# Taking the norms of q and k from squared slot-wise products, in an attention and expert kernel on one core

## The reference, cut to what matters

```python
def l2norm(t):
    n = jnp.linalg.norm(t, axis=-1, keepdims=True)
    return t / jnp.maximum(n, EPS)                       # EPS = 1e-12

q, k, v = (l2norm(q), l2norm(k), l2norm(v))              # 16 heads, DK = 16, DV = 64
attn = jnp.square(jax.nn.relu(jnp.einsum('bhid,bhjd->bhij', q, k)))
out = tanh_norm(jnp.einsum('bhij,bhjd->bhid', attn, v))  # tanh(n) * out / max(n, EPS)
return out.transpose(0, 2, 1, 3).reshape(b, n, h * d) @ Wout
```

## Time and profile before

| | |
|---|---|
| median of 3 runs | 552.65 us (552.19 to 552.93) |
| profiled execution, its own time | 551.87 us |
| its span in the trace | 549.8 us |
| busy: PE, DVE, ACT, POOL | 527.1, 425.2, 371.4, 331.3 us |
| attention | from 0 to about 219 us, then the experts |
| chain that ended last: PE, POOL, issue, DVE | 61%, 14%, 13%, 6% |

### The profile page before, as it was taken

One profiled execution on the slowest core, in us unless ns is written; L12 is line 12 of the kernel. 1 busy time (PEld: TensorE's weight loads), 2 busy tenths in 40 slices (PEclk: granted clock), 3 DMA queues, 4 the chain that ended last, 5 costly groups with the idle time before them and its releaser, 6 DMA issues.

```text
span 549.8 us, 10227 instructions
## 1 busy us (share of the span) xinstructions
PE 527.1 (96%) x3288; PEld 393.9 (72%) x3288; DVE 425.2 (77%) x1004; ACT 371.4 (68%) x682; POOL 331.3 (60%) x280
## 2 busy tenths in 40 slices
PE   8798899999999999898999999999999999999997
PEld 7565557676767666686878878878868878878884
DVE  5877868888978698669769778778769778777765
ACT  5697859687769786644565865865865865755654
POOL 6645919393947584395466655655655655665562
PEclk9899989999999999999999999999999999999999
DMA  7401010101010100660291760870760780771930
GB/s 218 131 2 30 1 30 1 32 1 30 2 31 1 30 2 9 171 148 2 77 209 30 184 153 4 176 156 11 184 151 4 182 175 5 170 159 35 214 83 20
DMA packets 37253, 44.75 MB, mean 81 GB/s; under 512 B 5840, under 2 KB 20304, under 8 KB 37200
## 3 DMA queue, kind: packets, MB, share of 16 engines
q1 hardware_dynamic: 32512, 42.40, 33.3%
q10 hardware_dynamic: 4688, 1.71, 1.3%
HBM read 40.94 MB, written 3.15 MB: 80 GB/s over the span
## 4 chain that ended last, share of the span: by engine, by line
PE 61%; POOL 14%; issue 13%; DVE 6%; ACT 4%; DMA 1%; SPq 0%; POOLq 0%; ACTq 0%; DVEq 0%
PE PS L1245 59%; POOL hl L517 11%; DVE aT L892 2%; ACT v L556 1%; POOL sr L446 1%; ACT rl L581 1%; DMA Osb<-wa_dram 1%; DVE n L871 1%; POOL mrstd L508 1%; POOL rstd L461 1%; DVE nmx L904 1%; ACT sqv L563 0%; POOL fxl L468 0%; DVE hb L1118 0%; PE PS L1338 0%
## 5 line engine op out<-in xcount | busy, mean ns | idle before, releaser
L517 POOL TENSOR_TENSOR hl<-hb,hh 128x512 fp32r<-128x512 f32 x127 | 164.3, 1295 | 129.2 <-ACT hh L735 124.9
L728 ACT ACTIVATE sil<-PS 128x512 f32<-128x512 f32 (+1 forms) x136 | 80.8, 595 | 79.0 <-PE PS L1245 72.4
L1113 DVE TENSOR_TENSOR PS<-sil,PS 128x512 f32<-128x512 f32 x128 | 88.3, 690 | 54.3 <-PE PS L1245 33.0
L1245 PE MATMUL PS<-fxh,wfh 128*128 128x512 f32 x264 | 104.9, 397 | 3.3 <-DVE hb L1118 2.9
L735 ACT ACTIVATE hh<-hb 128x512 fp32r<-128x512 f32 x128 | 80.3, 627 | 35.3 <-DVE hb L1118 33.4
L1245 PE MATMUL PS<-fxl,wfh 128*128 128x512 f32 x264 | 104.1, 394 | 0.0
L1245 PE MATMUL PS<-fxh,wfl 128*128 128x512 f32 x264 | 103.7, 393 | 0.0
L1118 DVE TENSOR_TENSOR hb<-PS,wbc 128x512 f32<-128x512 f32 x128 | 88.5, 691 | 12.9 <-issue 4.2
L892 DVE SCALAR_TENSOR_TENSOR aT<-PS,rl 128x1024 f32<-128x1024 f32 x64 | 75.2, 1216 | 14.7 <-ACT rl L581 14.6
L581 ACT ACTIVATE rl<-PS 128x1024 f32<-128x1024 f32 x64 | 62.8, 1050 | 21.7 <-PE PS L1245 21.7
L436 POOL TENSOR_TENSOR sr<-n2o,half 128x32 f32<-128x32 f32 x7 | 37.9, 5414 | 44.4 <-DVE n2o L899 44.4
(11 more groups left out here) (182 smaller groups left out, 900.1 us busy)
## 6 DMA issues: line engine op xcount, KB each, us to landing
wbc<-w_dram SPq DMA_DIRECT2D x48, 512.0 KB, 11.7
wbc<-w_dram SPq DMA_DIRECT2D x32, 128.0 KB, 3.0
wbc<-w_dram SPq DMA_DIRECT2D x16, 256.0 KB, 4.2
wfs<-wf_dram SPq DMA_DIRECT2D x32, 98.0 KB, 2.2
band_dram<-zero SPq DMA_DIRECT2D x16, 80.0 KB, 1.7
band<-band_dram ACTq DMA_DIRECT2D x4, 320.0 KB, 3.0
...
```

The lines of the kernel that those rows point to most:

```text
L517: g.tensor_tensor(hl[:, n % RING, :], hb[:, n % RING, :], hh[:, n % RING, :].bitcast(F32), ALU.subtract).then_inc(F("hl"), 1)
L728: s.activation(sil[0:rows, n % 2, :], PS[0:rows, G0 + n % 2, :], ACT.Silu).then_inc(F("silu"), 1)
L1113: v_.tensor_tensor(PS[:, bank, :], sil[:, n % 2, :], PS[:, bank, :], ALU.mult).then_inc(F("t"), 1)
L1245: return nc.tensor.matmul(o, w, m, start=start, stop=stop)
```

## The change

The token-wise second product of q and k is taken out, with its 512 columns of weights. The slot-wise products in `qk`, which are there anyway, are squared to a new buffer `sqg`: parts 0 and 1 by POOL (a multiplication of 128x512 each), part 2 by ACT. For the first batch DVE squares all three. PE's new `pair_sums(n)` adds them up over the rows of a head by eight matmuls with columns of ones (`indp`), into other columns of the same bank as the output's sums (`output_sums`, the former `norms`). One copy and one pair of transposes now carry the sums of q and k of batch n and of the outputs of batch n-2. `keep_norms` and `transpose_norms` therefore take the number n, and run once more at the start and once more at the end than before.

With that the order changes on every engine. PE's three `group` calls stand together after the first `score` of a pass; `values(n, 0, ...)` move one place later, `values(n, 1, ...)` to after the third `score`, `project(r, 0)` from before the third `score` to before the fourth. `qk` has two copies, so that a batch's parts may be written while the one before is in use. ACT puts the copies of q and k between the halves of a `relu`, and now does `keep_output(4b+1)` before `square_values(n, 0)`, and `square_values(n, 1)` before `keep_output(4b+2)`. DVE sums v's half 0 after the third `squares` of the pass instead of before it, and half 1 after the output's factors.

The floors change too: v's squares and the output's norm are floored by a maximum over pairs (`tensor_reduce`, one member of each pair a constant written once) in place of a `tensor_scalar`. `fill_idle` adds transposes of the identity with no use of their result: 4 before the first `score`, 10 and 8 at the start of passes 0 and 1, 10 before the last `score` of pass 1. The tokens of tiles 2 and 3 get a transfer of their own, ahead of the rest.

```diff
-        order += coming(n, ("qk", n, 0), ("qk", n, 1), ("v", n, 0, 0), ("v", n, 0, 1)) + late(q, ("nb", q))
-        order += coming(n, ("v", n, 1, 0)) + late(q, ("nt", q)) + coming(n, ("v", n, 1, 1))
-        order += ([("px", 0)] if b == B - 2 else []) + late(r, ("y", r, 0))
+        order += coming(n, ("g", n, 0), ("g", n, 1), ("g", n, 2)) + [("nb", n)]
+        order += coming(n, ("v", n, 0, 0), ("v", n, 0, 1)) + [("nt", n)] + ([("px", 0)] if b == B - 2 else [])
+        order += coming(n, ("v", n, 1, 0), ("v", n, 1, 1)) + late(r, ("y", r, 0))
...
+            def square_group(n, j):
+                pool.wait_ge(*freed("g", n, j))
+                pool.wait_ge(*full("nb", n - 1))
+                g.tensor_tensor(sqg[:, j, :], qk[:, n % 2, j, :], qk[:, n % 2, j, :], ALU.mult).then_inc(A("sqg_p"), 1)
...
             def keep_group(n, j):
                 act.wait_ge(*full("g", n, j))
-                after(act, A("S"), 2 * (NG * (n - 1) + (2 if j == 0 else NG)))
-                s.activation(qk[:, j, :], PS[:, bank_of("g", n, j), :], ACT.Copy).then_inc(free_of("g", n, j), 1)
+                after(act, A("S"), 2 * NG * (n - 1))
+                s.activation(qk[:, n % 2, j, :], PS[:, bank_of("g", n, j), :], ACT.Copy).then_inc(free_of("g", n, j), 1)
+
+            def square_group(n, j):
+                act.wait_ge(*freed("g", n, j))
+                act.wait_ge(*full("nb", n - 1))
+                s.activation(sqg[:, j, :], qk[:, n % 2, j, :], ACT.Square).then_inc(A("sqg_a"), 1)
+
...
-                relu(NG * b + 1)
+                relu_half(NG * b + 1, 0)
+                if more:
+                    keep_group(n, 0)
+                relu_half(NG * b + 1, 1)
                 if last:
                     prep_scores(0)
                 if more:
-                    square_pairs(n, 0)
-                    square_pairs(n, 1)
+                    keep_group(n, 1)
+                    keep_group(n, 2)
+                    square_group(n, 2)
                 keep_output(NG * b)
+                if last:
+                    keep_norms(n)
+                weight_high(NG * b)
+
+                relu_half(NG * b + 2, 0)
+                if more:
+                    keep_norms(n)
+                relu_half(NG * b + 2, 1)
...
                 if more:
                     keep_values(n, 0, 0)
                     keep_values(n, 0, 1)
-                if b:
-                    keep_norms(q)
-                weight_high(NG * b)
-
-                relu(NG * b + 2)
+                keep_output(NG * b + 1)
                 if more:
-                    keep_values(n, 1, 0)
-                    keep_values(n, 1, 1)
                     square_values(n, 0)
-                keep_output(NG * b + 1)
                 weight_high(NG * b + 1)
                 if b == B - 2:
                     prep_tokens(0)
...
 
                 relu(NG * b + 3)
                 if more:
+                    keep_values(n, 1, 0)
+                    keep_values(n, 1, 1)
                     square_values(n, 1)
-                    keep_group(n, 0)
-                    keep_group(n, 1)
                 keep_output(NG * b + 2)
-                if more:
-                    keep_group(n, 2)
...
+                v_.tensor_reduce(n2[:, n % 2, t, :, 0], sqv[:, :].rearrange("p (h d) -> p h d", d=DV),
                                  AX.X, ALU.add).then_inc(A("n2v"), 1)
-
-            def pair_norms(n, t):
-                dve.wait_ge(*freed("qk", n, t))
-                v_.tensor_reduce(n2[:, n % 3, t, 0:2 * H], sqqk[:, t, :].rearrange("p (h d) -> p h d", d=DK),
-                                 AX.X, ALU.add).then_inc(A("n2q"), 1)
-
-            def clear_norms(n, t):
                 dve.wait_ge(A("n2v"), 2 * n + t + 1)
-                dve.wait_ge(A("n2q"), 2 * n + t + 1)
-                v_.tensor_scalar(nm[:, n % 3, t, :], n2[:, n % 3, t, :], NORM_EPS * NORM_EPS, None, ALU.max).then_inc(A("nm"), 1)
-                dve.wait_ge(A("nm"), 2 * n + t + 1)
-                v_.reciprocal(rr[:, n % 3, t, :], nm[:, n % 3, t, 0:2 * H]).then_inc(A("rr"), 1)
+                v_.tensor_reduce(nv[:, n % 2, t, :], n2[:, n % 2, t, :, :], AX.X, ALU.max).then_inc(A("nv"), 1)
+
...
+            def pair_norms(n):
+                dve.wait_ge(*full("nt", n))
+                sums = PS[:, bank_of("nt", n), 0:2 * P].rearrange("p (i c x) -> p i c x", i=2, c=NG)
+                v_.tensor_scalar(nm[:, :, :].rearrange("p i (c x) -> p i c x", c=NG), sums[:, :, :, HG:3 * HG],
+                                 NORM_EPS * NORM_EPS, None, ALU.max).then_inc(free_of("nt", n), 1)
+                dve.wait_ge(*freed("nt", n))
+                v_.reciprocal(rr[:, n % 3, :, :], nm[:, :, :]).then_inc(A("rr"), 1)
...
-                v_.tensor_scalar(nmx[:, :, :], nn[:, :, :], NORM_EPS, None, ALU.max).then_inc(A("nmx"), 1)
+                v_.tensor_reduce(nmx[:, :, :], nn[:, :, :, :], AX.X, ALU.max).then_inc(A("nmx"), 1)
...
 
-                if b:
-                    if not last:
-                        for k in range(NG * q, NG * b):
-                            weight_low(k)
+                if b and more:
+                    for k in range(NG * q, NG * b):
+                        weight_low(k)
+                if last:
                     gather_norms(q)
                 squares(NG * b + 2)
                 if last:
                     choose_experts(0)
                     combine(0)
+                    add_attention(r, 0)
+                elif b:
+                    gather_norms(q)
+                if more:
+                    pair_norms(n)
+                if b == B - 4:
+                    prep_stats(0)
+                squares(NG * b + 3)
                 if more:
                     value_norms(n, 0)
-                    clear_norms(n, 0)
-                if b == B - 4:
-                    prep_stats(0)
-                if r >= 0:
-                    add_attention(r, 0)
-                squares(NG * b + 3)
+                if b:
+                    output_factors(q)
                 if more:
                     value_norms(n, 1)
-                    clear_norms(n, 1)
-                if b:
-                    output_factors(q)
+                    if r >= 0:
+                        add_attention(r, 0)
...
-            def norms(q):
-                pe.wait_ge(A("sqO"), NG * (q + 1))
-                bank, done = turn("nb", q)
+            def output_sums(n):
+                pe.wait_ge(A("sqO"), NG * (n - 1))
+                bank, done = turn("nb", n)
                 for s in range(2):
                     for g in range(NG):
                         last = mm(PS[SLOT * g:SLOT * (g + 1), bank, 0:L], ind[:, s, :], sqO[:, g, s * L:(s + 1) * L],
-                                  s == 0, s == 1)
+                                  s == 0, s == 1 and n >= B)
+                last.then_inc(A("nbo") if n < B else done, 1)
+
+            def pair_sums(n):
+                if n < 2:
+                    bank, done = turn("nb", n)
+                else:
+                    bank, done = turns.at["nb", n][0], full("nb", n)[0]
+                if n:
+                    pe.wait_ge(A("sqg_p"), 2 * n)
+                    pe.wait_ge(A("sqg_a"), n)
+                else:
+                    pe.wait_ge(A("sqg"), NQ)
+                    pe.wait_ge(cs("indp"), 1)
+                for g in range(NG):
+                    mm(PS[SLOT * g:SLOT * (g + 1), bank, 0:L], indp[:, 0, :],
+                       sqg[:, WQ_G[g] // 2, WQ_G[g] % 2 * L:(WQ_G[g] % 2 + 1) * L], n < 2, False)
+                for g in range(NG):
+                    last = mm(PS[SLOT * g:SLOT * (g + 1), bank, 0:L], indp[:, 1 + g % 2, :],
+                              sqg[:, 1, g // 2 * L:(g // 2 + 1) * L], False, True)
                 last.then_inc(done, 1)
 
-            def transpose_norms(q):
-                pe.wait_ge(*freed("nb", q))
-                bank, done = turn("nt", q)
...
+            def fill_idle(times, *job):
+                bank, k = turns.at[job]
+                after(pe, Z(f"free{bank}"), k - 1)
+                for _ in range(times):
+                    nc.tensor.transpose(PS[:, bank, 0:P], ident[:, :], ident[:, :])
...
+                if b < 2:
+                    fill_idle(10 if b == 0 else 8, "g", n, 0)
                 if b != 2:
                     score(NG * b + 1)
                 if r >= 0:
...
                     prep_turn_logits(0)
                 if more:
                     pe.wait_ge(*freed("xT", n))
-                    pairs(n, 0)
-                    pairs(n, 1)
+                    for j in range(NQ):
+                        group(n, j)
+                if b:
+                    output_sums(n)
                 attend(NG * b)
+
+                score(NG * b + 2)
                 if more:
+                    pair_sums(n)
                     values(n, 0, 0)
                     values(n, 0, 1)
-                if b:
-                    norms(q)
-
```

(19 more changed lines are left out.)

216 lines of the change are left out of this document (120 added, 96 removed).

## The result

The changed kernel takes 560.37 us (median of 6, 559.17 to 560.72), the kernel before 552.99 beside it (median of 6): a ratio of 1.0122, 95% interval 1.0094 to 1.0149. It is slower, by 7.4 us where 6.3 were forecast. The profiled execution spans 557.05 us, 7.2 more than before (549.84); its own time is 559.17.

The account below looks back on a forecast made before the run. The prediction took PE to bound the attention before the change, and the ACT and DVE stall after it. Terms 0 + 1.2 + 2.2 - 1.6 + 4.0 + 0.5 = +6.3 us gave 559.0 us, 8-in-10 range 547 to 565.

Parts of the forecast that it names:

- steps 1 to 6: Chain of ACT and DVE waits from the third `score` to the next pass's first: 14.15 us, PE alone 12.3.
- PE's own work: Middle pass by PE alone: 25.2 us, 0.8 less than before, if the other engines keep up.
- A: First to second `score` of a pass: 7.04 us by PE alone, 7.82 before.
- B: Second to third `score` of a pass: 5.9 us by PE alone, 6.97 before.
- C with D: Third `score` to the next pass's first: 12.3 us by PE alone, 14.15 with the stall, 11.28 before.
- The rival in which PE stays the bound: Middle passes: 1.9 us of unseen slack, so ACT need not stand; -8.6 us, 544 us; chance 0.11.
- steps 3 to 5: ACT's `sqv` waits for DVE's sum of half 0; `keep_output`, `th` and DVE's factors follow; last `squares` at R + 8.95.
- POOL's squares: POOL squares parts 0 and 1 at 1.30 us each, half a microsecond ahead of `pair_sums` in a middle pass.
- waits of pass 1: 0.45 us in A for POOL's scaling of v, 0.6 in B for POOL's squares; pass 1 26.8 us.
- The clock: Kept up in pass 2, PE's longest waits being 1.7 us; that pass 28.0 us against 29.6, -1.6.
- the rival in which my order is right and the clock falls too: Waits in the start and first passes lower the clock; +2 to +5 us, 561 to 564; chance 0.22.
- The floors: DVE's floor, 0.98 us beside POOL in a middle pass: its gain is hidden behind DVE's wait for `th`.

Follow-up runs that it names:

- Three experiments: On the changed kernel: two buffers for `sqv`, 555.79 us; square of half 1 later on ACT, 555.61 us; DVE's sum of half 0 before the third `squares`, 549.46 us.
- tanh first: "sum first" with ACT's tanh ahead of the square of half 1 and third `keep_output`, and more idle transposes: 545.58 us, ratio 0.9878 to the kernel before.
- run without fillings: Changed kernel without its 32 idle transposes: 561.2 us, ratio interval 1.0112 to 1.0191 to the kernel before.
- filled kernel before: Kernel before with idle transposes added at three places (10, 8 and 10), nothing else of the change: 550.2 us, ratio 0.9948.
- before, filled, floors: The filled kernel before with floors as maxima over pairs, also for q's and k's sums: 548.29 us, ratio 0.9914 to the kernel before.
- sum first: Changed kernel with DVE's sum of half 0 of v ahead of the third `squares` of a pass: 549.46 us, ratio 0.9942 to the kernel before.

## Why the prediction was right, and where it was not

**The stall, steps 1 to 6: right, each step within 0.11 us.** With R the start of the third `relu` and t that of the third `score`, in the pass shown: R at t + 2.29 (2.28 forecast); sum of half 0 at R + 3.34 (3.33); `sqv` at R + 4.66 (4.59); `th` at R + 6.58 (6.49); the fourth `attend` at R + 6.79 (6.7); `ff` at R + 6.91 (6.8); last `squares` at R + 9.00 (8.95); next first `score` at t + 14.21 (14.15). Three experiments that break the chain in three ways bring the pass to 25.6, 25.6 and 25.3, so the cause is shown. PE's wait before `attend` shows as "issue"; that it is the wait for `sqO` is read from the code and the times (`sqO` ends at 146.22, the `attend` starts at 146.32).

**PE's own work: right in sum.** A 6.99 (7.04 forecast; 7.13 with the tanh first), B 5.76 (5.9), C with D 12.02 where no wait is left, with the tanh first (12.3). A pass by PE alone is then 24.91, 25.2 in the forecast. What the change promises is 1.16 us a pass. The rival in which PE stays the bound had nearly this price, but its condition, slack in steps 3 to 5, is not there: it takes two orders that the change does not have.

**POOL's squares and the waits of pass 1: too dear.** I priced the squares at 1.30 us each by the earlier trace rows; two take 2.04 (129.31 to 131.35), and the sums begin 1.2 us after them. In pass 1 they end at 51.01 and the sums begin at 51.32, so B had none of the 0.6 us waiting; nor had A the 0.45 I gave it for POOL's scaling of v. Pass 1 came out at 25.65, 1.15 under the forecast, almost all of it by these two waits. They are the terms of the attention most mis-sized.

**The clock: not as I took it.** From the rows of before I read that a wait of 1.55 us brings no fall where 1.92 does. In the changed kernel it fell at 39.08, within a wait of 1.71, with one of 1.25 just before:

```profile
36.43 1.15 PE L1290 MATMUL PS<-qk 32*128 32x256 f32 x16 [1.25 <-DVE aT L948]
37.50 0.44 PE L1310 MATMUL PS<-ident,xnA 128*128 128x128 f32 x2
39.65 3.33 PE L1290 MATMUL PS<-aT,v 128*64 128x256 f32 x16 [1.71 <-issue]
```

The `attend` took 3.33 us in place of 1.95. C with D of pass 0 took 13.35 us for the 12.6 forecast; in the run without fillings, with the same two waits and no fall there, it took 12.68, so about 0.7 is the clock's. In pass 1 the same two waits (at 61.85 and 65.07) brought no fall, and in the run without fillings it was the other way round: no fall behind them in pass 0, one in pass 1. So which wait does it can't be told from its length here. In this the rival in which my order is right and the clock falls too came true by half, at 0.7 us and not at 2 to 5. Nor was a fall as dear as I took it from the rows: filled, passes 0 and 2 of the kernel before gave back 0.8 and 2.5 us, where that rival has 1.6 and 3.5. Pass 2 itself, 27.96, came as forecast (28.0), with the clock kept; it is 27.97 in the run without fillings, so they are not shown to be what kept it.

**The floors: hidden in the change, as forecast,** since DVE waits 1.40 us for `th` in any case. In the filled kernel before, which is without that stall, they are worth 0.15 us a middle pass and 0.66 in pass 1.

**The end: a step left out.** I took the last pass and the experts at nothing. They cost 2.1 us more, 1.2 of it by the one `comb`. The attention was forecast 1.2 too dear and this 2.1 too cheap, and so the sum came out only 0.9 low; that it came so near is in part luck, and the mechanism rests on the steps above and not on the sum. From the start of pass 7 to the end, the traces without a fall there take 348.2 us (before, filled, floors) to 351.8 (tanh first), though the experts' code is the same. That this is a matter of which small steps meet is shown for the `comb` alone; the rest stays open, and I have no way to forecast that part from a trace with another start.

## What to carry to other kernels

Before an instruction is moved behind another, look at who waits for its result and what is queued behind that waiter: 1.21 us of DVE's work, placed after instead of before an idle stretch of 2.33, held ACT, and through it PE and DVE again, and turned a saving of 0.75 us a pass (1.16 with the tanh moved too) into a loss of 0.9. Look for such a stretch of idle time on the engine first; here it took only two lines to use it. Where small steps of two engines meet by chance, an operation that the other engine did not hold (here `tensor_reduce`, 0.25 us beside POOL) is worth more than one that is shorter when alone (`tensor_scalar`, 0.19 alone and 0.98 beside POOL).

## What the runs showed of the chip

- A DVE instruction may be held until POOL's ends, whole: the floor 0.98 us in place of 0.19, `ff` 1.65 in place of 0.19, `comb` 1.21 in place of 0.29, each ending within 0.15 us of the POOL instruction beside it. The Trainium skill, "SBUF — State Buffer", "Who interferes with whom", says that a DVE instruction with two SBUF inputs contends with a POOL instruction that reads SBUF, that kinds such as `tensor_scalar` can contend, and that `tensor_reduce` never does on this chip. The traces agree for these three and for the `tensor_reduce` floor, 0.25 us beside POOL. They do not agree that every POOL instruction which reads SBUF holds such a one: through POOL's power `vi`, 2.89 us from 115.43 on in the filled kernel, `f<-rec,rr` at 115.81, with two SBUF inputs, took its usual 0.19.
- POOL's multiplication of a 128x512 float32 buffer by itself takes 1.02 to 1.04 us; the difference of two buffers to fp32r takes 1.30.
- PE without earlier work runs at half pace at first (products of 512 columns 0.43 us apart until 12.1 us). Idle transposes alone brought it to full pace, at 4.94 us in the changed kernel. A printed granted clock of 1.00 ahead of the trace's first record of the clock says nothing; the distance from start to start does.
- The granted clock of one kernel falls in some executions and not in others (mean 0.986 to 1.000 in the ten of "sum first"). Short idle transposes in the waits made both the clock and the time more even: in the kernel before, 549.5 to 550.6 us with them against 551.1 to 555.7 without.
